# Attention products of both sequences merged and moved amid the experts in a fused two-layer tower

## The chip, the cores and the metric

The kernel runs on one core of one Trainium2 chip. The metric is the device time of one execution in microseconds, the median of several runs.

## The reference

Sixteen sequences of 128 tokens (D = 256) go through an embedding and two layers. All arithmetic is in float32.

```python
h = emb[ids] + 0.1 * sum_d mask_d * (base @ W_exp[d].T) @ W_proj[d].T     # 8 domains
n = layernorm(h)
c_kv = n @ W_dkv.T                      # latents, 128 wide
q    = n @ W_dq.T @ W_uq.T              # 16 heads of 16
h += softmax(causal(q . k_eff . c_kv / 4)) @ c_kv @ v_eff
n = layernorm(h)
h += sum_e gate_e(n) * (n @ expert_w[e]) + bias                           # 8 experts, threshold 0.1
n = layernorm(h)
u = conv4(n) @ in_w.T + in_b ; dt = tanh(n @ dt_w.T + dt_b) @ tr_w.T
s_t = silu(s_(t-1) + dt_t + ...)        # a recurrence over the 128 steps
h += out_w(s + u)
h += fp4_linear(silu(fp4_linear(layernorm(h), w_gate)) * fp4_linear(.., w_up), w_down)
```

## The kernel before, in words

**Stages.** The sequences are worked off in eight pairs (`u` = 0, 1 within a pair). A software pipeline overlaps two of them: `body(i)` runs the *back* part of pair `i` (scores, softmax, attention, gate, experts, up to the third layer norm) together with the *front* part of pair `i + 1` (embedding correction, first layer norm, latents, queries, keys, values). `body(-1)` has the front alone, `body(0)` both, `body(1)` to `body(6)` are one hardware loop and have besides the recurrence inputs of the pair before (`rec`), `body(7)` has no front; TensorE transposes feed-forward weights in its place. After the pairs come the recurrence over 128 steps and the quantized feed-forward.

**Order.** There is no planner. Each engine has its own list of calls, written out by hand, and runs its instructions in that order; semaphores order the engines among each other. An instruction that waits holds all that stand behind it on its engine.

**TensorE (L579 to L888).** In the order of a looped pair: for `u` = 0 and 1 the transposes of the next pair's raw rows `x_tok` (L575, called at L760), which wait for GpSimd's copy (`base_copied`) and for the values of the pair before; `scores(0)` for the first sequence (32 products, L597, and four causal masks, L601); `expand(0)`; `recurrence_inputs()` (L694), which waits for the convolution; half of `scores(1)`, `expand(1)`, the other half; `delta` (L711), transposes of the probabilities (L611) between those of the masked rows; `attend` (L624) with `project` between; the transposes of `n_tok`; `compress(0)` (L732: latents for queries and for keys and values of one sequence); then the gate input (L575), gate and four expert groups for each sequence (L657), each followed by the bias product (L670). Last come `compress(1)`, `heads` four times (L719: queries and keys of each sequence), `values(0)`, the transpose of the second sequence's third norm `n3_tok` and `values(1)` (L725).

**PSUM.** Four banks hold scores, probabilities and expert outputs (`pq`), two the back part (`pback`), and two the front part (`pfront[0]`, `pfront[1]`): in `before` sequence `u` uses `pfront[u]`. `scores(0)` and the expert groups wait until VectorE has read the quarter (`moe_read`).

**ScalarE (L986 to L1134)** copies from PSUM to SBUF: `xT`, `nT`, `latT`, queries, keys (two copies each, by the parity of the head), `n3T`; and it computes the 32 exps of each pair's head groups (L999) behind VectorE's maxima, and the tanh `dt_act` (L1027).

**VectorE (L1307 to L1543).** Row maxima (L1315), masking of the expanded rows (L1474), `projected` (L1400) and `deltas` (L1409, L1411) for the recurrence inputs, copies of transposed probabilities (L1321), the sum of the embedding correction (L1505), layer norm statistics (L1292, L1296) and their application (L1304), the expert mix (L1375, L1377 to L1386) and the first half of the convolution (L1421, L1424). In looped pairs it also quantizes one piece of the feed-forward weights in ten steps `weights(0)` to `weights(9)` (L1447 to L1468) that are strewn between the rest. `attend(u, 0)` on TensorE waits for `d_stored`, which `deltas` signals.

**GpSimd (L445 to L483)** has, in this order in each body: the copies of the next pair's `hidden` rows to `x_tok` (L455), the other half of the convolution (L438, L443), and for each layer norm two small steps, the sum (L425) and the power (L428) that give `rstd`. The last of them in a body is that of the third norm of the second sequence, `rstd_of(2, 1, ...)`, and the copies to `x_tok` of the next body stand behind it. In `body(0)` GpSimd also issues the gathers of the embedding rows of all later pairs between these steps.

Of the kernel before, what the change touches and what calls it, by code (L numbers as in the profile page):

```python
# [29 lines left out]
T = 128  # L30
# [44 lines left out]
def tower(nc, ids, domain_map, emb_table, w_expand, w_project, w_dq, w_uqT, w_dq_rows, w_dkv,  # L75
# [3 lines left out]
    with ctx:  # L79
# [67 lines left out]
        nT = sb("nT", [128, 2, KD, T])  # L147
        latT = sb("latT", [LATENT, 2, 2, T])
# [407 lines left out]
        def _(pe):  # L556
# [22 lines left out]
            def body(i, front, back, rec):  # L579
# [92 lines left out]
                def recurrence_transposed(u):  # L672
                    pe.wait_ge(ln_norm[2], n[u])
                    transposes(pback[u], n3_tok[:, u, :]).then_inc(xn3T_done, 1)
# [19 lines left out]
                def recurrence_inputs():  # L694
                    pe.wait_ge(n3T_ready, sequences(pe, i, 0))
                    for k in range(KD):
# [4 lines left out]
                        projected = mm(pback[0][0:STATE, 0:2 * T], inw_sb[:, k, :],  # L701
                                       mixed[:, k, :, :].rearrange("p u t -> p (u t)"),
                                       start=(k == 0), stop=(k == KD - 1), skip_group_check=True)
                        ranks = mm(pback[0][STATE:STATE + RANK, 0:2 * T], dtw_sb[:, k, :],
                                   n3T[:, :, k, TAPS - 1:], start=(k == 0), stop=(k == KD - 1), skip_group_check=True)
                    projected.then_inc(in_done, 2)
                    ranks.then_inc(rank_done, 2)
# [7 lines left out]
                def heads(u, ready, w, x, done):  # L715

                    pe.wait_ge(ready, fn[u])
                    for c in range(KD):
                        last = mm(pfront[u][:, c * T:(c + 1) * T], w[:, c * 128:(c + 1) * 128], x,  # L719
                                  start=True, stop=True)  # L720
                    last.then_inc(done, 1)

                def values(u):
                    pe.wait_ge(k_ready, fn[u])
                    mm(pfront[u][:, 0:D], latT[:, u, 1, :], veff_sb[:], start=True, stop=True).then_inc(v_done, 1)  # L725

                def compress(u):

                    pe.wait_ge(nT_ready, fn[u])
                    for c, w in enumerate((wdq_sb, wdkv_sb)):  # L730
                        for k in range(KD):
                            last = mm(pfront[u][:, c * T:(c + 1) * T], w[:, k, :], nT[:, u, k, :],  # L732
                                      start=(k == 0), stop=(k == KD - 1))
# [62 lines left out]
                if front:  # L796
                    expand(1)
                if not front:
                    weights_transposed(1)
                if back:  # L800
                    scores(1, (2, 3))
                    if rec:
                        delta(0, 2, 1, pback[1])
# [3 lines left out]
                    probs_transposed(0, 0)  # L807
                if front:
# [3 lines left out]
                if front:  # L812
                    masked_transposed(1)
                if back:
# [31 lines left out]
                if front:  # L846
                    compress(0)
# [3 lines left out]
                if back:  # L851
# [9 lines left out]
                    expert_bias(0)  # L861
                    gate(1)
                    experts(1, 0)
                    experts(1, 1)
# [20 lines left out]
                if last_pair:  # L885
# [79 lines left out]
        def _(act):  # L965
# [20 lines left out]
            def body(i, front, back, rec):  # L986
# [34 lines left out]
                def recurrence_transposed(u):  # L1021
                    act.wait_ge(xn3T_done, n[u])
# [8 lines left out]
                def queries(u):  # L1031

                    act.wait_ge(q_done, fn[u])
                    copy(qT[:, u].rearrange("p g t -> p (g t)"), pfront[u][:, 0:D], q_ready, scale=HS ** -0.5)

                def keys(u):
                    act.wait_ge(k_done, fn[u])
                    for r in (0, 1):
                        last = nc.scalar.activation(kT[:, u, r].rearrange("p g t -> p (g t)"), pfront[u][:, 0:D],
                                                    ACT.Identity, scale=of_parity[:, r:r + 1])  # L1040
                    last.then_inc(k_ready, 1)
# [16 lines left out]
                if front:  # L1058
                    for u in (0, 1):
                        act.wait_ge(baseT_done, fn[u])  # L1060
                        copy(xT[:, u].rearrange("p k t -> p (k t)"), pfront[u][:, 0:D], xT_ready)
# [20 lines left out]
                def compressed(u):  # L1082
                    act.wait_ge(lat_done, fn[u])
                    copy(latT[:, u].rearrange("p k t -> p (k t)"), pfront[u][:, 0:D], lat_ready)
# [30 lines left out]
                if back:  # L1115
                    gate_input(0)
                    gate(0)
                    gate_transposed(0)
                    gate_input(1)
                    gate(1)  # L1120
                    gate_transposed(1)
# [3 lines left out]
                if front:  # L1125
                    compressed(1)
                    queries(0)
                    queries(1)
                    keys(0)
                    keys(1)  # L1130
                if back:
                    recurrence_transposed(1)
                if last_pair:
# [87 lines left out]
        def _(dve):  # L1221
# [85 lines left out]
            def body(i, front, back, rec):  # L1307
# [119 lines left out]
                def values(u):  # L1427
                    dve.wait_ge(v_done, fn[u])
                    V.tensor_copy(v_aug[:, u, :, 0:HS],
                                  pfront[u][:, 0:D].rearrange("p (h d) -> p h d", h=HEADS)).then_inc(v_ready, 1)  # L1430
# [47 lines left out]

                if rec:
# [250 lines left out]
```

## Time and profile before

| | us |
|---|---|
| median of 3 runs | 634.71 (633.86 to 637.6) |
| profiled execution | 637.28 |
| its span, first to last instruction | 635.3 |
| TensorE matmul busy | 547.1 (86%) |
| VectorE busy | 454.4 (72%) |
| ScalarE busy | 252.2 (40%) |
| GpSimd busy | 215.3 (34%) |
| mean granted TensorE clock | 0.945 of 2.4 GHz |

The pairs take the span from about 14 to 440 us, the recurrence and the feed-forward the rest. Starts of instructions are in microseconds from the span's start. TensorE's ends are modelled, so differences of starts say more than ends. A float32 product shows as two instructions.

### The profile page before, as it was taken

To read this page: it belongs to the slowest core of one execution; us is meant where nothing else is said; L and a number is where in the kernel's file an instruction comes from. 1 tells how busy PE (TensorE), PEld (TensorE's weight loads), DVE (VectorE), ACT (ScalarE), POOL (GpSimd) and SP (SyncE) were. 2 spreads that over 40 slices of the span, in tenths; PEclk is the share of its full clock that TensorE was granted. 3 is DMA by queue.
4 is the path that set the end of the run, shared out by engine and by line. 5 is a ranking of instruction groups with operands and counts; after the bars stand their busy time and mean duration, and the time that the engine had idled before them with its cause. 6 is when DMAs were issued, how large, how long until landed. Compare 5 with 4: busy or idle time off the path is not lost.

```text
span 635.3 us, 9416 instructions
## 1 busy us (share of the span) xinstructions
PE 547.1 (86%) x3062; PEld 331.1 (52%) x3062; DVE 454.4 (72%) x1120; ACT 252.2 (40%) x781; POOL 215.3 (34%) x412
## 2 busy tenths in 40 slices
PE   2888969999998998998998998993569998989884
PEld 2665445555555555655645644741235555555553
DVE  1254757778778788788787786486678898988852
ACT  1263026326326326316416515802335444443321
POOL 6406561222213213114114113021347767664110
PEclk9879889999999999999999998996579999999997
DMA  6800100000000000000000000003300000000000
GB/s 189 248 2 27 34 25 1 2 0 0 0 0 0 0 0 0 0 0 0 0 0 0 0 0 2 1 2 68 64 1 10 17 8 18 9 18 17 9 17 17
DMA packets 13517, 12.75 MB, mean 20 GB/s; under 512 B 2795, under 2 KB 12724, under 8 KB 13492
## 3 DMA queue, kind: packets, MB, share of 16 engines
q1 hardware_dynamic: 12212, 10.34, 6.1%
q0 software_dynamic: 1280, 2.11, 1.2%
q8 instruction: 12, 0.20, 0.1%
q14 instruction: 13, 0.11, 0.1%
HBM read 8.25 MB, written 2.10 MB: 16 GB/s over the span
## 4 chain that ended last, share of the span: by engine, by line
PE 54%; DVE 12%; issue 10%; ACT 9%; POOL 8%; SPq 4%; DMA 2%; DVEq 0%; POOLq 0%; ACTq 0%
PE psum L657 13%; PE psum L919 8%; PE psum L941 5%; ACT probs L999 4%; PE psum L597 4%; SPq L383 3%; PE psum L739 3%; PE psum L575 2%; POOL rstd L428 2%; PE psum L601 2%; PE psum L750 2%; PE psum L719 2%; DVE stats L1292 2%; POOL rstd L425 2%; PE psum L732 1%
## 5 line engine op out<-in xcount | busy, mean ns | idle before, releaser
L657 PE MATMUL psum<-expw_sb,n2T 128*128 128x512 f32 x256 | 119.1, 609 | 0.0
L425 POOL TENSOR_TENSOR rstd<-meanvar,ln_eps_col 128x1 f32<-128x1 f32 x64 | 17.8, 278 | 288.2 <-DVE meanvar L1296 288.1
L919 PE MATMUL psum<-wguT,n2T 128*128 128x512 f32 (+1 forms) x192 | 82.8, 583 | 0.0
L999 ACT ACTIVATE probs<-psum,neg_max 128x128 f32<-128x128 f32 x256 | 69.1, 391 | 33.4 <-DVE neg_max L1315 33.3
L657 PEld LDWEIGHTS psum<-expw_sb,n2T 128*128 128x128 f32 x256 | 47.2, 194 | 47.6 <-issue 47.6
L941 PE MATMUL psum<-wdT,probsT 128*128 128x256 f32 x192 | 50.3, 405 | 12.7 <-ACT probsT L967 12.7
L919 PEld LDWEIGHTS psum<-wguT,n2T 128*128 128x128 f32 x192 | 38.1, 200 | 39.5 <-issue 34.4
L1315 DVE TENSOR_REDUCE neg_max<-psum 128x4 f32<-128x512 f32 x64 | 40.4, 681 | 19.7 <-PE psum L601 19.7
L967 ACT ACTIVATE probsT<-psum 128x512 f32<-128x512 f32 x72 | 37.2, 530 | 30.6 <-PE psum L611 26.0
L1143 ACT ACTIVATE probs<-u_now 64x16 f32<-64x16 f32 x128 | 27.4, 214 | 53.9 <-POOL u_now L517 37.9
L941 PEld LDWEIGHTS psum<-wdT,probsT 128*128 128x128 f32 x192 | 35.2, 196 | 25.8 <-issue 21.0
L1377 DVE SCALAR_TENSOR_TENSOR acc<-psum,g_w,acc 128x256 f32<-128x256 f32 x96 | 42.0, 479 | 7.7 <-PE psum L657 3.1
L517 POOL TENSOR_TENSOR u_now<-probs,drive 64x16 f32<-64x16 f32 x87 | 37.1, 427 | 30.0 <-ACT probs L1143 30.0
L611 PE MATMUL psum<-ident,probs 128*128 128x128 f32 x256 | 39.0, 283 | 2.6 <-ACT probs L999 2.6
L1304 DVE TENSOR_SCALAR n_tok<-hidden,meanvar,rstd 128x256 f32 (+1 forms) x48 | 20.1, 420 | 27.1 <-POOL rstd L428 27.1
L575 PE MATMUL psum<-ident,n_tok 128*128 128x128 f32 x128 | 25.2, 288 | 15.8 <-DVE n_tok L1304 11.7
L428 POOL TENSOR_TENSOR rstd<-rstd,minus_half 128x1 f32<-128x1 f32 x64 | 36.0, 562 | 5.0
L498 POOL TENSOR_TENSOR hq<-wgu_tmp,hsc 128x704 f32<-128x704 f32 x16 | 22.4, 1398 | 36.7 <-DVE wgu_tmp L1254 36.6
L597 PE MATMUL psum<-kT,qT 32*128 32x128 f32 x512 | 30.1, 298 | 4.7 <-ACT probs L999 2.4
L611 PEld LDWEIGHTS psum<-ident,probs 128*128 128x128 f32 x256 | 28.7, 143 | 10.1 <-issue 6.0
L575 PEld LDWEIGHTS psum<-ident,n_tok 128*128 128x128 f32 x128 | 15.1, 143 | 33.2 <-DVE n_tok L1304 15.5
L597 PEld LDWEIGHTS psum<-kT,qT 32*128 32x128 f32 x512 | 25.6, 200 | 12.8 <-issue 12.8
(172 smaller groups left out, 1025.7 us busy)
## 6 DMA issues: line engine op xcount, KB each, us to landing
expw_sb<-in_expert_w SPq DMA_DIRECT2D x8, 256.0 KB
expw_sb<-hidden SPq DMA_DIRECT2D x16, 128.0 KB
result<-res SPq DMA_DIRECT2D x16, 128.0 KB
w_raw<-in_w_down SPq DMA_DIRECT2D x1, 704.0 KB, 9.4
w_raw<-in_w_gate SPq DMA_DIRECT2D x1, 640.0 KB, 7.1
w_raw<-in_w_up SPq DMA_DIRECT2D x1, 640.0 KB, 8.2
wexp_sb<-in_w_expand SPq DMA_DIRECT2D x1, 256.0 KB, 3.1
wproj_sb<-in_w_project SPq DMA_DIRECT2D x1, 256.0 KB, 3.2
```

The source lines that it names most:

```text
L428: pool.tensor_tensor(rstd[:, k, u, :], rstd[:, k, u, :], minus_half[:], ALU.pow).then_inc(ln_rstd[k], 1)
L517: pool.tensor_tensor(u_now[:], gated_all[:, t, :], drive[:, t, :], ALU.add).then_inc(u_ready, 1)
L575: last = nc.tensor.transpose(bank[:, k * 128:k * 128 + rows], src[:, k * 128:(k + 1) * 128], ident[:])
L597: mm(pq[:, g, j * T:(j + 1) * T], qT[g * GROUP:(g + 1) * GROUP, u, j // 2, :], kT[g * GROUP:(g + 1) * GROUP, u, j % 2, j // 2, :], start=( ...
L611: last = nc.tensor.transpose(pq[:, g, j * T:(j + 1) * T], probs[:, u, HPQ * g + j, :], ident[:])
L657: last = mm(pq[:, g, :], n2T[:, u, k, :], expw_sb[:, k, EPQ * g:EPQ * (g + 1), :].rearrange("p e n -> p (e n)"), start=(k == 0), stop=(k = ...
L919: last = mm(pgu[u][:, c0:c1], xqT[:, u, k, :], wguT[:, k, c0:c1], start=(k == 0), stop=(k == KD - 1))
L941: last = mm(pdown, hqT[0:rows, u, k, :], wdT[0:rows, k, :], start=(k == 0), stop=(k == KI - 1))
L967: nc.scalar.activation(dst, src, ACT.Copy, **kw).then_inc(s, 1)
L999: last = nc.scalar.activation(probs[:, u, h, :], pq[:, g, j * T:(j + 1) * T], ACT.Exp, bias=neg_max[:, u, h:h + 1])
L1315: V.tensor_reduce(neg_max[:, u, HPQ * g:HPQ * (g + 1)], pq[:, g, :].rearrange("p (h k) -> p h k", h=HPQ), AX.X, ALU.max, negate=True).then ...
L1377: last = V.scalar_tensor_tensor(out=a[:, u, :], in0=p, scalar=g_w[:, u, e:e + 1], in1=a[:, u, :], op0=ALU.mult, op1=ALU.add)
```

## The change

The front part's products take both sequences at once. `compress(x, w)` makes the query latents (`x` = 0) or the key and value latents (`x` = 1) of both sequences in bank `pfront[x]`; `heads` makes queries or keys of both; `values` both sequences' values in one bank. They stand at other places of TensorE's list: the second compress behind the third expert group of the first sequence, the query heads behind its bias, the key heads behind the first expert group of the second sequence; only `values` stays at the end. ScalarE's copies (512 columns each) and VectorE's value copy follow. Both `x_tok` transposes go to `pfront[1]` and one copy takes both. The transpose of the second sequence's `n3_tok` and its copy move, in looped pairs and the last, behind `scores(0)` of the next body; the ranks' products are split from the projection's, which goes behind the first transpose of probabilities; `expand(1)` goes before `scores(1)`. On VectorE `maxima(0)` comes ahead of the convolution, `projected`, `deltas` and `weights(0)` move back, `weights(6)` ahead of the application of the first gate norm, `weights(9)` ahead of that of the second, and `values` behind `mix(1)`. GpSimd's list is as before.

```diff
@@ TensorE
-                def heads(u, ready, w, x, done):
-                    pe.wait_ge(ready, fn[u])
+                def heads(x, w, done):
+                    pe.wait_ge(lat_ready, fn[x])
                     for c in range(KD):
-                        last = mm(pfront[u][:, c * T:(c + 1) * T], w[:, c * 128:(c + 1) * 128], x, ...
+                        last = mm(pfront[x][:, 2 * c * T:2 * (c + 1) * T], w[:, c * 128:(c + 1) * 128],
+                                  latT[:, x].rearrange("p u t -> p (u t)"), start=True, stop=True)
+                def values():
+                    pe.wait_ge(lat_ready, fn[1])
+                    pe.wait_ge(q_ready, fn[1])
+                    for u in (0, 1):
+                        last = mm(pfront[0][:, u * D:(u + 1) * D], latT[:, 1, u, :], veff_sb[:], ...
+                def compress(x, w):
+                    pe.wait_ge(nT_ready, fn[1])
+                    for k in range(KD):
+                        last = mm(pfront[x][:, 0:2 * T], w[:, k, :], nT[:, :, k, :], ...
                 def expand(u):
                     pe.wait_ge(xT_ready, fn[u])
+                    if u == 0:
+                        wait(pe, v_ready, fbefore)
...
                 if front:
+                    wait(pe, k_ready, fbefore)
                     for u in (0, 1):
                         pe.wait_ge(base_copied, fn[u])
-                        wait(pe, v_ready, later(pe, fbefore, u - 1))
-                        transposes(pfront[u], x_tok[:, u, :]).then_inc(baseT_done, 1)
+                        transposes(pfront[1][:, u * D:(u + 1) * D], x_tok[:, u, :]).then_inc(baseT_done, 1)
                 if back:
                     scores(0, range(QUARTERS))
+                if rec:
+                    recurrence_transposed(1, behind=1)
                 if front:
                     expand(0)
                 if rec:
-                    recurrence_inputs()
+                    ranks_behind()
+                if front:
+                    expand(1)
                 if back:
                     scores(1, (0, 1))
-                if front:
-                    expand(1)
                     scores(1, (2, 3))
-                    if rec:
-                        delta(0, 2, 1, pback[1])
                     probs_transposed(0, 0)
+                if rec:
+                    inputs_behind()
                 if front:
                     masked_transposed(0)
                     probs_transposed(0, 1)
                     masked_transposed(1)
+                if rec:
+                    delta(0, 2, 1, pback[1])
...
-                    compress(0)
+                    compress(0, wdq_sb)
...
                     experts(0, 0)
                     experts(0, 1)
                     experts(0, 2)
+                if front:
+                    compress(1, wdkv_sb)
                     gate_transposed(0)
                     gate_input(1)
                     experts(0, 3)
                     expert_bias(0)
+                if front:
+                    heads(0, wuqT_sb, q_done)
                     gate(1)
                     experts(1, 0)
+                if front:
+                    heads(1, keff_sb, k_done)
                     experts(1, 1)
...
                 if front:
-                    compress(1)
-                    heads(0, lat_ready, wuqT_sb, latT[:, 0, 0, :], q_done)
-                    heads(1, lat_ready, wuqT_sb, latT[:, 1, 0, :], q_done)
-                    heads(0, q_ready, keff_sb, latT[:, 0, 1, :], k_done)
-                    heads(1, q_ready, keff_sb, latT[:, 1, 1, :], k_done)
-                    values(0)
-                if back:
+                    values()
+                if last_pair:
                     recurrence_transposed(1)
-                if front:
-                    values(1)
@@ ScalarE
+                    act.wait_ge(baseT_done, fn[1])
+                    nc.scalar.activation(xT[:].rearrange(...), pfront[1], ACT.Copy).then_inc(xT_ready, 2)
+                if rec:
+                    recurrence_transposed(1, behind=1)
...
                     gate(0)
+                    compressed(1)
                     gate_transposed(0)
                     gate_input(1)
+                    queries()
                     gate(1)
+                    keys()
@@ VectorE
+                if back:
+                    maxima(0, range(QUARTERS))
                 if rec:
                     convolved(0, 0, 2, 1, conv_dve, TAPS * i - TAPS)
-                if back:
-                    maxima(0, range(QUARTERS))
                 if front:
                     expanded(0)
-                if rec:
-                    projected(0, 2, 1)
-                    weights(0)
                     maxima(1, (0, 1))
                     expanded(1)
                     maxima(1, (2, 3))
+                    probs_out(0, 0)
+                    if rec:
+                        projected(0, 2, 1)
+                    probs_out(0, 1)
+                    weights(0)
                     if rec:
                         deltas(0, 2, 1, pback[1])
-                    for g in range(3):
-                        probs_out(0, g)
+                    probs_out(0, 2)
...
                     attention_out(0)
                     weights(5)
+                    weights(6)
                     ln_apply(1, 0, n[0], seq(hidden, i, 0), n2_tok[:, 0, :])
-                    weights(6)
                     weights(7)
...
                     attention_out(1)
                     weights(8)
+                    weights(9)
                     ln_apply(1, 1, n[1], seq(hidden, i, 1), n2_tok[:, 1, :])
...
                     mix(1)
+                    if front:
+                        values()
...
                     ln_apply(2, 1, n[1], seq(hidden, i, 1), n3_tok[:, 1, :])
-                if front:
-                    values(0)
-                    values(1)
-                if back:
-                    weights(9)
```

## Rows read from the trace of the kernel before

**Rows 1.** Windows, one period: us, then PE, PEld, DVE, ACT, POOL, clock, DMA

```profile
166.47:215.24 48.77, 45.58 (x308) 27.43 (x308) 38.75 (x97) 20.76 (x64) 11.60 (x21) 1.00 0.00 0
```

**Rows 2.** Timeline, TensorE: start, us, engine, line, operation, tiles, count [idle before, releaser]

```profile
174.23 0.44 PE L575 MATMUL psum<-ident,n_tok 128*128 128x128 f32 x2 [0.56 <-DVE n_tok L1304]
...
184.90 0.69 PE L670 MATMUL psum<-expb_sb,wT 8*128 8x256 f32 x2
...
186.52 1.35 PE L719 MATMUL psum<-latT,wuqT_own 128*128 128x128 f32 x8
...
190.56 0.43 PE L575 MATMUL psum<-ident,x_tok 128*128 128x128 f32 x2
...
191.87 1.17 PE L597 MATMUL psum<-kT,qT 32*128 32x128 f32 x32 [0.17 <-issue]
...
193.85 1.03 PE L739 MATMUL psum<-wexp_sb,xT 128*128 128x256 f32 x4
...
205.79 0.43 PE L624 MATMUL psum<-probsT,v_aug 128*32 128x128 f32 x8
...
215.24 0.44 PE L575 MATMUL psum<-ident,n_tok 128*128 128x128 f32 x2 [0.52 <-DVE n_tok L1304]
```

**Rows 3.** Timeline, VectorE, the same period

```profile
183.17 2.83 DVE L1377 SCALAR_TENSOR_TENSOR acc<-psum,g_w,acc 128x256 f32<-128x256 f32 x6
...
188.09 0.18 DVE L1296 BATCH_NORM_AGGREGATE meanvar<-stats 128x2 f32<-128x6 f32 x1
...
192.68 2.33 DVE L1424 SCALAR_TENSOR_TENSOR mixed<-n3T,convw_sb,mixed 128x256 f32<-128x256 f32 x3
194.94 2.47 DVE L1315 TENSOR_REDUCE neg_max<-psum 128x4 f32<-128x512 f32 x4
...
198.15 0.85 DVE L1447 TENSOR_REDUCE w_sc<-w_raw 128x44 f32 x1
...
203.96 1.87 DVE L1321 COPY probsT<-psum 128x512 f32<-128x512 f32 x3
...
207.46 0.42 DVE L1505 SCALAR_TENSOR_TENSOR hidden<-psum,hidden 128x256 f32 x1
```

**Rows 4.** Timeline, GpSimd, the seam between two pairs

```profile
188.35 0.19 POOL L425 TENSOR_TENSOR rstd<-meanvar,ln_eps_col 128x1 f32<-128x1 f32 x1 [7.29 <-DVE meanvar L1296]
188.62 0.55 POOL L428 TENSOR_TENSOR rstd<-rstd,minus_half 128x1 f32<-128x1 f32 x1
189.12 0.80 POOL L455 COPY x_tok<-hidden 128x256 f32 x2
```

**Rows 5.** Timeline, ScalarE, the exps

```profile
195.65 3.21 ACT L999 ACTIVATE probs<-psum,neg_max 128x128 f32<-128x128 f32 x12 [3.53 <-DVE neg_max L1315]
...
199.38 3.22 ACT L999 ACTIVATE probs<-psum,neg_max 128x128 f32<-128x128 f32 x12
```

**Rows 6.** Timeline, VectorE's weight steps and GpSimd's norm step beside one

```profile
166.33 0.52 DVE L1462 TENSOR_SCALAR w_mag<-w_mag 128x704 f32<-128x704 f32 x1
...
172.15 0.89 DVE L1466 TENSOR_TENSOR wgu_tmp<-wgu_tmp,w_mag 128x704 f32<-128x704 f32 x1
...
172.31 0.78 POOL L425 TENSOR_TENSOR rstd<-meanvar,ln_eps_col 128x1 f32<-128x1 f32 x1 [6.34 <-DVE meanvar L1296]
```

**Rows 7.** Timeline, TensorE's long stalls in pairs 0, 1 and 7

```profile
38.57 1.16 PE L597 MATMUL psum<-kT,qT 32*128 32x128 f32 x16 [1.60 <-issue]
...
92.00 1.11 PE L575 MATMUL psum<-ident,x_tok 128*128 128x128 f32 x4 [5.46 <-POOL x_tok L455]
93.04 2.09 PE L597 MATMUL psum<-kT,qT 32*128 32x128 f32 x32
...
390.21 0.62 PE L701 MATMUL psum<-mixed,inw_sb 128*64 128x256 f32 x2 [2.39 <-DVE mixed L1424]
```

**Rows 8.** Windows, the clock behind two of them

```profile
40.00:44.00 4.00, 4.00 (x23) 2.93 (x22) 1.71 (x3) 2.72 (x11) 0.00 (x0) 0.52 0.00 2
...
392.00:393.00 1.00, 1.00 (x4) 0.13 (x2) 0.80 (x2) 1.00 (x6) 0.00 (x0) 0.50 0.00 0
```

More of the change, by code:

```diff
@@ L670, in expert_bias, with recurrence_transposed @@
                     mm(pback[u][:, 0:D], wT[:, u, :], expb_sb[:], start=True, stop=True).then_inc(bias_done, 1)
-                def recurrence_transposed(u):
-                    pe.wait_ge(ln_norm[2], n[u])
+                def recurrence_transposed(u, behind=0):
+                    pe.wait_ge(ln_norm[2], before if behind else n[u])
                     transposes(pback[u], n3_tok[:, u, :]).then_inc(xn3T_done, 1)
@@ L692, in project_in, with ranks_behind, inputs_behind @@
                     last.then_inc(in_done, 1)
-                def recurrence_inputs():
+                def ranks_behind():
                     pe.wait_ge(n3T_ready, sequences(pe, i, 0))
+                    for k in range(KD):
+                        last = mm(pback[0][STATE:STATE + RANK, 0:2 * T], dtw_sb[:, k, :],
+                                  n3T[:, :, k, TAPS - 1:], start=(k == 0), stop=(k == KD - 1), skip_group_check=True)
+                    last.then_inc(rank_done, 2)
+                def inputs_behind():
                     for k in range(KD):
@@ L700, in recurrence_inputs @@
                             pe.wait_ge(conv_pool, conv_steps(pe, i, POOL_STEPS, 0))
[L701 to L707, printed above, removed]
+                        last = mm(pback[0][0:STATE, 0:2 * T], inw_sb[:, k, :],
+                                  mixed[:, k, :, :].rearrange("p u t -> p (u t)"),
+                                  start=(k == 0), stop=(k == KD - 1), skip_group_check=True)
+                    last.then_inc(in_done, 2)
                 def delta(u0, u1, behind, bank):
@@ L713, in delta @@
                        start=True, stop=True, skip_group_check=True).then_inc(delta_done, u1 - u0)
-                def heads(u, ready, w, x, done):
-                    pe.wait_ge(ready, fn[u])
+                def heads(x, w, done):
+                    pe.wait_ge(lat_ready, fn[x])
                     for c in range(KD):
[L719 to L733, printed above, removed]
+                        last = mm(pfront[x][:, 2 * c * T:2 * (c + 1) * T], w[:, c * 128:(c + 1) * 128],
+                                  latT[:, x].rearrange("p u t -> p (u t)"), start=True, stop=True)
+                    last.then_inc(done, 2)
+                def values():
+                    pe.wait_ge(lat_ready, fn[1])
+                    pe.wait_ge(q_ready, fn[1])
+                    for u in (0, 1):
+                        last = mm(pfront[0][:, u * D:(u + 1) * D], latT[:, 1, u, :], veff_sb[:], start=True, stop=True)
+                    last.then_inc(v_done, 2)
+                def compress(x, w):
+                    pe.wait_ge(nT_ready, fn[1])
+                    for k in range(KD):
+                        last = mm(pfront[x][:, 0:2 * T], w[:, k, :], nT[:, :, k, :],
+                                  start=(k == 0), stop=(k == KD - 1))
                     last.then_inc(lat_done, 1)
@@ L1019, in gate_transposed, with recurrence_transposed @@
                     copy(wT[:, u, :], pback[u][0:EXPERTS, 0:T], wT_ready)
-                def recurrence_transposed(u):
-                    act.wait_ge(xn3T_done, n[u])
+                def recurrence_transposed(u, behind=0):
+                    act.wait_ge(xn3T_done, before if behind else n[u])
                     copy(n3T[:, u, :, TAPS - 1:], pback[u][:, 0:D].rearrange("p (k t) -> p k t", k=KD), n3T_ready)
@@ L1058, in body @@
                 if front:
-                    for u in (0, 1):
-                        act.wait_ge(baseT_done, fn[u])
-                        copy(xT[:, u].rearrange("p k t -> p (k t)"), pfront[u][:, 0:D], xT_ready)
+                    act.wait_ge(baseT_done, fn[1])
+                    nc.scalar.activation(xT[:].rearrange("p u k t -> p (u k t)"), pfront[1], ACT.Copy).then_inc(xT_ready, 2)
+                if rec:
+                    recurrence_transposed(1, behind=1)
                 if back:
@@ L1080, in attended, with compressed @@
                     copy(yT[:, u].rearrange("p c t -> p (c t)"), pback[u][:, :], yT_ready)
-                def compressed(u):
-                    act.wait_ge(lat_done, fn[u])
-                    copy(latT[:, u].rearrange("p k t -> p (k t)"), pfront[u][:, 0:D], lat_ready)
+                def compressed(x):
+                    act.wait_ge(lat_done, fn[x])
+                    copy(latT[:, x].rearrange("p u t -> p (u t)"), pfront[x][:, 0:2 * T], lat_ready)
                 def masked_transposed(u):
@@ L1425, in convolved, with values @@
                                                    op0=ALU.mult, op1=ALU.add).then_inc(steps, 1)
[L1427 to L1430, printed above, removed]
+                def values():
+                    dve.wait_ge(v_done, fn[1])
+                    V.tensor_copy(v_aug[:, :, :, 0:HS],
+                                  pfront[0].rearrange("p (u h d) -> p u h d", u=2, h=HEADS)).then_inc(v_ready, 2)
                 def weights(k):
@@ L1535, in body @@
                         deltas(1, 2, 0, pfront[1])
[L1536 to L1540 removed]
                 if not back:
+                    values()
                     taps()
```

35 lines of the change are left out of this document (19 added, 16 removed).

## The prediction

> **What bounds the kernel now.** Read the windows of one period of the loop first: from one pair's gate input to the next is 48.77 us, and TensorE is busy for 45.58 of them at the full clock (2.4 GHz), VectorE for 38.75 [rows 1]. So TensorE is the bound, but VectorE is not far off. Then the timeline of TensorE over that period: the places where it waits are 0.56 us before the second gate input, 0.52 us before the first, and some tenths around the end of the pair [rows 2]. Then VectorE's timeline, for what its chain does when TensorE gets ahead [rows 3], and that of GpSimd, which stands between the end of one pair and the start of the next [rows 4].
>
> The seam is what the change touches. Today `mix(1)` ends on VectorE at 186.0 (183.17 + 2.83), the aggregate of its layer norm at 188.27 [rows 3], GpSimd's power at 189.17, and only then, from 189.12, does GpSimd copy the next pair's rows to `x_tok`, 0.40 us each [rows 4]. TensorE comes to the transposes of `x_tok` at 190.56, about a microsecond after the first copy, since it has 5 us of compress, heads and values to do after the last bias (184.90) [rows 2]. That work is the cover of the chain mix, norm, power, copy.
>
> **The change part by part.**
>
> 1. Merged products. 16 head products of 128 columns are two groups of 1.35 us; four of 256 columns are 1.03 us [rows 2] (each product shows as two instructions). So the heads go from 2.7 to 2.1 us, compress from as much to 2.1, values stay at about 1.05. A gain of 0.6 to 1.0 us of TensorE's time, waits for ScalarE between the heads included.
>
> 2. Moved amid the experts: one compress and two heads, 3 x 1.03 = 3.1 us. The 0.56 us wait before the second gate input hides about 0.3 of it (not all: item 5). So the last expert group of the pair ends at 184.9 + 2.8 = 187.7 instead of 184.9 [rows 2].
>
> 3. What follows on the path. `mix(1)` needs that group: two products of 0.47 us behind it [rows 3], so it ends at 188.65, not 186.0. From there to the aggregate 2.27 us as before (190.9), to the end of the power 0.90 (191.8) [rows 3, 4], and then the copies to `x_tok`, ready at 192.2 and 192.6. GpSimd's order isn't changed. TensorE has only the bias (0.6) and values (1.0) left behind its experts and stands at the `x_tok` transposes at 189.3. It waits 3.0 us, and `scores(0)` stands behind the transposes in its queue: it starts at 192.95, where it starts at 191.87 now. This is +1.1 us a pair, and the cover that hid it is the very work that moved.
>
> 4. Scores to attend. Now VectorE does the convolution (most of it in 2.33 us) before `maxima(0)` at 194.94, and exps start at 195.65 [rows 3, 5]. Afterwards the maxima come first, but the second recurrence transpose, its copy on ScalarE (0.4) and their hand-overs stand behind `scores(0)` and ahead of the exps. So: `scores(0)` ends 195.05, transpose and copy to 195.85, exps from 195.85. Twelve exps 3.2, the tanh 0.5, four exps 1.1 [rows 5]: 200.6. VectorE: maxima to 196.8, convolution 3.05 to 199.85, `expanded(0)` 0.4, so `maxima(1)` begins at 200.2 and ScalarE waits for it till 200.85; exps end at 205.2. VectorE then has maxima to 203.45 (behind `scores(1)`, which ends at 202.15), a copy (0.63), `projected` (about 0.6, taken as a copy), a copy, `weights(0)` 0.85 and `deltas` 0.7: 206.9. `attend(0,0)` waits for `deltas` and starts at 206.95 against 205.79 now [rows 2, 3]. What goes out with the old order (TensorE's short waits for the convolution, an expand between the score halves) is used up by these waits. Third copy and weights 1 to 4 (0.6 + 1.7) put VectorE at the projection's sum at 209.2, where it is at 207.46 now: +1.7 us [rows 3]. From there VectorE's chain leads: sums, norm, attention out, the norm of the gate input. 0.15 us of a wait for TensorE is saved: +1.55.
>
> 5. `weights(6)` before the first gate norm and `weights(9)` before the second. They now run while VectorE would wait for GpSimd's power. But beside `weights(8)` (0.89 us) GpSimd's first step takes 0.78 us and ends with it, where alone it takes 0.19 [rows 6, 4]. So the power can be held the same way beside `weights(6)` (0.52 [rows 6]). I bound this by 0 (it has read its input) and 0.5 us (it waits out the whole instruction) and take 0.25, the middle, on the path: +1.8 us a pair. Beside `weights(9)`, as long as `weights(8)`, it may cost 0.7, of which the inserted compress hides all but about 0.3; that is the part not gained in item 2.
> The Trainium skill, "SBUF — State Buffer", section "Who interferes with whom", says that a VectorE instruction with two SBUF inputs or in a 2-port mode and a GpSimd instruction that reads SBUF exclude each other for the whole instruction. The stretched row agrees. By that rule item 5 would cost 0.45 and the forecast would be 1 us higher.
>
> 6. The clock. A stall of 3.0 us a pair is not only its own length. From pair 0 on TensorE stalled for over 1.5 us five times in this trace; the rows show the first, the third and the fourth. Behind the 1.60 us at 38.57 the granted clock is 0.52 from 40 to 44, behind the 2.39 us at 390.21 it is 0.50 from 392 to 393, and behind the 5.46 us at 92.00 `scores(0)` takes 2.09 us for its 32 products, against 1.17 [rows 7, 8, 2]. That is the lower of its two levels, 1.2 GHz. The short waits of the period don't do this: its clock is 1.00 [rows 1]. So I expect the half clock behind the new stall, where `scores(0)` (0.92 more for the products, about 0.8 for the masks, the same ratio) and the transpose stand on the path. Bounds: 0, if it falls elsewhere or doesn't come, and 3.4, if the expands and the second scores are slowed too (a stretch at 1.2 GHz covers 7 us from 40 on). I take 1.6, nearest to `scores(0)` alone.
> The Trainium skill, "TensorE: Matmul & The Clock Gate", section "HAM oscillation — how this bites in real kernels", names only longer gaps than this as what lets the clock fall. The row of 2.39 us speaks against that; by the rule the forecast would be the second case below.
>
> **Sum.** Per period 1.8 + 1.6 = +3.4 us; five periods lie between pair 1's gate input and pair 6's: +17.0. Before them: in pair 0, `expand(1)` fills the 1.60 us wait and the half clock behind it goes (40 to 44 and on), -2.5; the inserted 3.1 us delay the last power of pair 0, behind which GpSimd issues its last gathers, and TensorE already waits 5.46 us for the copy behind those, +3.1 in full; and pair 1's steps of items 4 and 5 (which has the half clock already) +1.3. That is +1.9. In the last pair there are no `x_tok` transposes: `scores(0)` starts 1.3 us sooner, and exps no longer wait for the convolution (TensorE's 2.39 us there [rows 7]). `weights(0)` is absent too. I work out `attend(0,0)` 1.6 us sooner; bounds 0 and 3: -1.6. Together +17.3 us. The profiled execution took 637.28 (span 635.3), the median of the runs is 634.71; the same difference on the median gives 652.0.
>
> **The rivals.**
> - Stall without the half clock: 5 x 1.8 + 1.9 - 1.6 = +9.3, 644.0. For it: that how the stall falls counts (0.3 to 0.6 us waits do nothing). Against it: even 1.60 us did. Chance 0.17.
> - The clock falls and also slows the experts, since TensorE waits again, 1.2 us, at the first gate input. Experts are wholly TensorE's: up to 5.2 a period in all, +26, 661 and above. Chance 0.10, at the upper edge.
> - The seam's loss is made good: with maxima first, exps start 1 us sooner after `scores(0)`, and if `maxima(1)` isn't held by the convolution (were VectorE's 3.05 us near 1.9, as four steps of the 0.47 us in `mix` [rows 3] would be), +1.1 is met by -1.1: 636, within 1%. Against: GpSimd's own convolution runs at the same time, as now. Chance 0.12.
> - Faster: `scores(0)` isn't held by the copies. Then it starts at 189.85, 2.0 us sooner; half of it is lost to VectorE's order, 1.0 a period stays: -5 -1.6 -1 = -7.6, 627. It decides at one point: `x_tok` has to be copied by 189.3, 3 us before mix, norm and power allow. Against it is the order of GpSimd's queue, for it that the merged products could be much shorter than 1.03 us (they'd have to be nearly nothing). That the change doesn't act as it says is a part of this. Chance 0.08.
>
> **How the numbers follow.** The forecast, stall with half clock, has 0.53: 645 to 661. With 0.17, 0.10, 0.12 and 0.08 for the rivals: faster by over 1% 0.08, within 1% 0.12, slower 0.80 (1% is about what a measurement tells from no change). Range 638 to 662: it leaves out the faster case and most of the clock in the experts.
>
> **What would show it.** In the profile after: a wait of TensorE's transposes of `x_tok` (L575) for GpSimd's copy (L455) of about 3 us in each of the looped pairs; no such wait before the last pair. Granted clock 0.5 for some microseconds behind it. ScalarE idle about 0.3 us ahead of the fifth quarter's exps; attend waiting for `drive`. Period 52.2 us (50.6 without the clock). It is wrong if the transposes wait for under 1 us, if the period is below 49.5, or if the experts' stretch is not 2.8 us longer.

## Result and profile after

The changed kernel takes 655.56 us (median, 653.02 to 656.88), the one before 634.29 in the same series: ratio 1.034 (1.029 to 1.039), slower, as forecast (652.0, 638 to 662). Profiled executions: 656.56 against 637.28 us, +19.3; medians: +21.3. Over all series the kernel before ran in 628.6 to 640.9 us, and the ratios leave out runs of more than 1.5% above the fastest of their kernel.

TensorE over one looped pair, the timeline (start, duration, line, tiles, count, idle before and releaser), to be held against [rows 2]:

```profile
171.15 0.44 PE L576 MATMUL psum<-ident,n_tok 128*128 128x128 f32 x2 [0.92 <-DVE n_tok L1325]
...
178.08 1.03 PE L740 MATMUL psum<-nT,wdkv_sb 128*128 128x256 f32 x4
...
179.58 0.44 PE L576 MATMUL psum<-ident,n_tok 128*128 128x128 f32 x2 [0.36 <-DVE n_tok L1325]
...
192.37 0.69 PE L671 MATMUL psum<-expb_sb,wT 8*128 8x256 f32 x2
192.99 1.13 PE L733 MATMUL psum<-veff_sb,latT 128*128 128x256 f32 x4
196.92 1.12 PE L576 MATMUL psum<-ident,x_tok 128*128 128x128 f32 x4 [2.80 <-POOL x_tok L456]
197.96 2.09 PE L598 MATMUL psum<-kT,qT 32*128 32x128 f32 x32
...
207.63 1.16 PE L598 MATMUL psum<-kT,qT 32*128 32x128 f32 x16 [0.66 <-ACT probs L1015]
...
213.82 0.43 PE L625 MATMUL psum<-probsT,v_aug 128*32 128x128 f32 x8 [0.43 <-DVE drive L1432]
...
223.69 0.44 PE L576 MATMUL psum<-ident,n_tok 128*128 128x128 f32 x2 [0.93 <-DVE n_tok L1325]
```

Behind the bias and `values` TensorE is done at 194.1 and stands before the `x_tok` transposes until 196.92. `scores(0)` behind them takes 2.09 us for its 32 products. What it waited for is in VectorE's and GpSimd's timelines [rows 3, 4]:

```profile
192.48 0.88 DVE L1398 SCALAR_TENSOR_TENSOR acc<-psum,g_w,acc 128x256 f32<-128x256 f32 x2 [1.17 <-PE psum L658]
...
195.43 0.18 DVE L1317 BATCH_NORM_AGGREGATE meanvar<-stats 128x2 f32<-128x6 f32 x1
```

```profile
195.69 0.19 POOL L426 TENSOR_TENSOR rstd<-meanvar,ln_eps_col 128x1 f32<-128x1 f32 x1 [9.28 <-DVE meanvar L1317]
195.96 0.55 POOL L429 TENSOR_TENSOR rstd<-rstd,minus_half 128x1 f32<-128x1 f32 x1
196.47 0.80 POOL L456 COPY x_tok<-hidden 128x256 f32 x2
```

VectorE waited 1.17 us for the last expert group (before it was behind, not waiting), then came mix, norm, power and copy. The waits of TensorE, summed (us, times, longest), say that one place grew:

```profile
PE psum L576 <- POOL x_tok L456: 23.3, 6, 9.3
PE psum L957 <- ACT probsT L983: 12.4, 16, 0.8
PE psum L576 <- DVE n_tok L1325: 11.9, 15, 1.7
```

Before, the first of these was 5.5 us, once. Now it is 9.3 us in that same place, in the body of pair 1, where the copy waits for the last gathers, and 2.8 us in each of the five looped pairs behind it. Last the windows, one for each of the five periods (TensorE, its weights, VectorE, ScalarE, GpSimd busy, then the granted clock), and of three stretches in them, to be held against [rows 1]:

```profile
117.48:171.15 53.67, 48.27 (x292) 28.19 (x292) 38.55 (x96) 20.10 (x60) 12.03 (x21) 0.94 0.00 0
171.15:223.69 52.54, 47.31 (x292) 28.12 (x293) 38.43 (x96) 19.98 (x60) 12.03 (x21) 0.94 0.00 0
223.69:277.23 53.54, 48.12 (x293) 28.27 (x293) 38.74 (x96) 20.19 (x60) 11.91 (x21) 0.94 0.00 0
277.23:329.76 52.53, 47.18 (x292) 28.04 (x293) 38.41 (x96) 19.88 (x60) 12.04 (x21) 0.94 0.00 0
329.76:383.39 53.63, 49.16 (x292) 28.96 (x293) 38.38 (x96) 19.75 (x60) 12.03 (x21) 0.90 0.00 0
...
154.00:157.00 3.00, 3.00 (x20) 1.93 (x17) 1.98 (x4) 2.54 (x11) 0.00 (x0) 0.61 0.00 0
196.00:202.00 6.00, 5.08 (x42) 3.38 (x43) 2.05 (x5) 0.60 (x1) 1.27 (x3) 0.50 0.00 0
...
329.76:335.00 5.24, 5.20 (x17) 2.88 (x18) 3.23 (x13) 0.74 (x3) 0.00 (x0) 0.73 0.00 0
```

The period is 53.18 us in the mean against 48.77, and the clock 0.94 and less in every period, where it was 1.00. From 196 to 202, around the end of the stall, it is at the lower level (1.2 GHz) throughout. In the last period the start of the experts is slowed too (0.73 from 329.76 to 335.00), although TensorE works nearly without a gap there. TensorE's busy time rises by 1.6 to 3.6 us a period (45.58 to between 47.18 and 49.16) though there are fewer instructions: a part of the work runs at half the clock.

### The profile page after: what moved, and what is told of

The parts are those of the page before. It is cut to its first block, busy times and chain, and to the rows that moved or that the text cites. A ratio compares the mean times of both kernels' runs of the same rounds, so it can differ in the third digit from the quotient of the medians.

```text
span 654.6 us, 9150 instructions
## 1 busy us (share of the span) xinstructions
PE 551.4 (84%) x2934; PEld 329.7 (50%) x2934; DVE 452.4 (69%) x1112; ACT 245.9 (38%) x749; POOL 217.2 (33%) x412
## 4 chain that ended last, share of the span: by engine, by line
PE 48%; DVE 15%; issue 12%; ACT 10%; POOL 8%; SPq 4%; DMA 2%; POOLq 0%; DVEq 0%; ACTq 0%
PE psum L658 14%; PE psum L935 7%; ACT probs L1015 5%; PE psum L957 5%; PE psum L598 3%; SPq L384 3%; PE psum L576 3%; POOL rstd L429 3%; PE psum L724 2%; PE psum L602 2%; DVE stats L1313 2%; PE psum L612 2%; POOL rstd L426 2%; DVE n_tok L1325 1%; PE psum L646 1%
## 5 line engine op out<-in xcount | busy, mean ns | idle before, releaser
L658 PE MATMUL psum<-expw_sb,n2T 128*128 128x512 f32 x256 | 121.0, 612 | 0.0
L429 POOL TENSOR_TENSOR rstd<-rstd,minus_half 128x1 f32<-128x1 f32 x64 | 41.8, 653 | 5.0
L598 PE MATMUL psum<-kT,qT 32*128 32x128 f32 x512 | 34.3, 343 | 6.2 <-ACT probs L1015 4.9
L598 PEld LDWEIGHTS psum<-kT,qT 32*128 32x128 f32 x512 | 29.2, 239 | 14.5 <-issue 14.5
L612 PEld LDWEIGHTS psum<-ident,probs 128*128 128x128 f32 x256 | 30.8, 149 | 8.5 <-issue 7.6
```

Source lines behind the costliest of these rows:

```text
L429: pool.tensor_tensor(rstd[:, k, u, :], rstd[:, k, u, :], minus_half[:], ALU.pow).then_inc(ln_rstd[k], 1)
L598: mm(pq[:, g, j * T:(j + 1) * T], qT[g * GROUP:(g + 1) * GROUP, u, j // 2, :], kT[g * GROUP:(g + 1) * GROUP, u, j % 2, j // 2, :], start=( ...
L612: last = nc.tensor.transpose(pq[:, g, j * T:(j + 1) * T], probs[:, u, HPQ * g + j, :], ident[:])
L658: last = mm(pq[:, g, :], n2T[:, u, k, :], expw_sb[:, k, EPQ * g:EPQ * (g + 1), :].rearrange("p e n -> p (e n)"), start=(k == 0), stop=(k = ...
```

## Experiments

Each kernel is the changed one with the edit shown, if not said otherwise. Results are medians and ratios to the kernel before in the same series.

**Copies first.** GpSimd's last norm step of a looped pair goes behind the next pair's copies (in pair 7's body its own stays where it was):

```diff
                 if rec:
+                    rstd_of(2, 1, before)
                     convolved(i, 1, 0, 2)
...
-                    rstd_of(2, 1, n[1])
+                    if not front:
+                        rstd_of(2, 1, n[1])
```

> The changed kernel with one edit on GpSimd: in looped pairs the last norm step of the pair before is issued behind the copies to x_tok instead of ahead of them. Theory (the seam: TensorE waits 2.8 us for the copies, and the half clock follows from that wait): the wait goes, scores(0) starts 3 us sooner in the period at the full clock, VectorE's order then gives a part of it back; period 48 to 49 us instead of 53.2, time 628 to 636. Rival (the loss lies in VectorE's new order and in the convolution and the copy behind scores(0)): TensorE then waits at the third norm's transpose instead, about as long, and the time stays above 648.

Measured: 627.49 us, 0.989 (0.985 to 0.993). TensorE's timeline at the seam, and the windows of a period:

```profile
185.69 0.60 PE L578 MATMUL psum<-ident,x_tok 128*128 128x128 f32 x4
186.22 1.17 PE L600 MATMUL psum<-kT,qT 32*128 32x128 f32 x32
187.33 1.04 PE L604 MATMUL psum<-causal_bf,ident_bf 128*128 128x512 bf16 x4
188.75 0.44 PE L578 MATMUL psum<-ident,n_tok 128*128 128x128 f32 x2 [0.39 <-DVE n_tok L1327]
```

```profile
162.88:210.87 47.99, 44.96 (x293) 26.53 (x293) 38.75 (x96) 19.89 (x60) 11.71 (x21) 1.00 0.00 0
```

The wait is gone, `scores(0)` covers the norm all but 0.39 us, and the clock stays full. The order of the norm step and the copies in GpSimd's queue was 28 us, 26 of them in the five periods (53.18 against 47.97 in the mean). Without it the rest of the change gains 1.1% on the median, a little more than expected. The kernel before ran in 629.1 to 640.9 us in this series, so against its fastest run the gain is only 1.6 us. The rival, that VectorE's order is the loss, falls.

**Products in the stall.** The wait stays, but TensorE works in it:

```diff
                     wait(pe, k_ready, fbefore)
+                    if rec:
+                        for _ in range(10):
+                            mm(pfront[1], ident_bf[:], causal_bf[:].rearrange("p h q -> p (h q)"),
+                               start=True, stop=True)
```

> The changed kernel with ten bf16 products of 512 columns (masks into a free bank, results unused, about 2.4 us) in the place of TensorE's wait for x_tok, in the looped pairs. The wait for the copy stays as long in sum (2.8 us), only TensorE isn't idle in it. Theory (half of the loss is the clock that falls behind the stall): no stretch at half clock behind the seam, period 53.2 down to 50.8, time 655.6 down by 11 to 14, 642 to 645. Rival (the clock falls only behind longer gaps, or for other reasons): no gain, 654 to 658.

Measured: 646.0 us, 1.021 (1.015 to 1.028), 9.6 us less than the changed kernel for 60 products more. `x_tok` comes as late as ever; TensorE still idles 0.64 us. The windows of two periods:

```profile
167.55:217.93 50.38, 47.15 (x302) 27.59 (x302) 38.21 (x96) 19.95 (x60) 11.98 (x21) 1.00 0.00 0
217.93:269.98 52.05, 48.79 (x303) 28.28 (x303) 38.44 (x96) 20.16 (x60) 11.97 (x21) 0.97 0.00 0
```

Four of the five periods are 50.4 us at the full clock, one fell to half for a while: 50.73 in the mean, and 646.0 is 1 us above what was expected. So of the 4.41 us by which a period of the changed kernel is longer than before, 1.6 (50.4 against 48.77) are waiting and order and 2.8 (53.18 against 50.4) are the clock. What pulled the clock down was TensorE's idleness in the stall, not the change's instructions; that it also falls without such a stall, the second window shows.

**Weights back.** `weights(6)` and `weights(9)` at their old places:

```diff
                     weights(5)
-                    weights(6)
                     ln_apply(1, 0, n[0], seq(hidden, i, 0), n2_tok[:, 0, :])
+                    weights(6)
...
                     weights(8)
-                    weights(9)
                     ln_apply(1, 1, n[1], seq(hidden, i, 1), n2_tok[:, 1, :])
...
+                if back:
+                    weights(9)
```

> The changed kernel with weights(6) and weights(9) at their old places. Theory (a VectorE instruction on SBUF holds up GpSimd's power beside it: 0.84 and 1.21 us instead of 0.55): both powers take 0.55 again, the first gate input comes 0.3 us sooner and TensorE's 0.36 us wait before the second goes: 0.65 us a period in six periods, -4 us, 651.5. If only the start matters (the instruction waits for its turn anyway): under 1 us. Both weight steps then run in VectorE's other gaps and cost nothing.

Measured: 645.52 us, 1.020 (1.013 to 1.027): -10, not -4. GpSimd's powers and the weight steps beside them in the changed kernel, then the powers with the weights back:

```profile
169.72 0.53 DVE L1483 TENSOR_SCALAR w_mag<-w_mag 128x704 f32<-128x704 f32 x1
169.81 0.84 POOL L429 TENSOR_TENSOR rstd<-rstd,minus_half 128x1 f32<-128x1 f32 x1
...
177.77 0.89 DVE L1489 TENSOR_TENSOR w_raw<-wgu_tmp,w_sc 128x704 f32 x1
177.87 1.21 POOL L429 TENSOR_TENSOR rstd<-rstd,minus_half 128x1 f32<-128x1 f32 x1
```

```profile
168.15 0.55 POOL L429 TENSOR_TENSOR rstd<-rstd,minus_half 128x1 f32<-128x1 f32 x1
...
175.90 0.55 POOL L429 TENSOR_TENSOR rstd<-rstd,minus_half 128x1 f32<-128x1 f32 x1
```

The mechanism holds: both powers were held up, by 0.29 and 0.66 us. The Trainium skill, "SBUF — State Buffer", section "Who interferes with whom", has this rule (the two exclude each other for the whole instruction). The rows agree in that both powers end only behind the weight step beside them; by the rule I had reckoned 0.45 for the first, and the row says 0.29. But the time fell by more than twice the forecast. Periods are 51.64 and 50.81 us in turn, each with one stretch at half clock, a long and a short one. The changed kernel has periods of 52.54 with one long stretch and of 53.6 with two short ones (the second is the 0.61 from 154 to 157 above). Like against like, the long stretch costs 0.9 us less than 52.54, near the 0.65 expected; the rest is that no period has a second stretch. Why it is gone was not tried by itself.

**Merged in place.** `compress(1)`, `heads` and their copies back at the end of the pair, merged:

```diff
                     experts(0, 2)
-                if front:
-                    compress(1, wdkv_sb)
...
                     expert_bias(0)
-                if front:
-                    heads(0, wuqT_sb, q_done)
...
                     experts(1, 0)
-                if front:
-                    heads(1, keff_sb, k_done)
...
                 if front:
+                    compress(1, wdkv_sb)
+                    heads(0, wuqT_sb, q_done)
+                    heads(1, keff_sb, k_done)
                     values()
```

> The changed kernel with compress(1), both heads and their copies back at the end of the pair: merged for both sequences, but not amid the experts. Theory (the place costs, not the merge): the last expert group ends 2.8 us sooner in the period, so mix, norm and copies do too, and TensorE arrives at x_tok with the copies ready or within 0.5 us of it; no half clock; period 48.0 to 48.8, time 626 to 634. Rival (the merged products or VectorE's order cost): above 645.

Measured: 631.55 us, 0.998 (0.995 to 1.001). The windows:

```profile
162.33:210.70 48.37, 44.66 (x292) 26.73 (x292) 38.19 (x96) 20.06 (x60) 11.92 (x21) 1.00 0.00 0
```

The period is 48.5 in the mean, the clock full. Merging takes 0.9 us off TensorE's busy time (45.58 before [rows 1]), of which the period keeps 0.25 (48.77 before), and costs nothing; the place amid the experts, with the order of GpSimd's queue, is the loss.

**Third norm in its pair.** The second recurrence transpose and its copy on ScalarE are turned back, ahead of the `x_tok` transposes (TensorE's list is shown):

```diff
-                if rec:
-                    recurrence_transposed(1, behind=1)
...
                 if front:
                     values()
+                if back:
+                    recurrence_transposed(1)
```

> The changed kernel with the second recurrence transpose and its copy back at the end of their own pair, between values and the transposes of x_tok; all else as changed. Theory: it waits for the norm that is ready just before the copies are, so the stall is as long (2.6 to 3.0 us, now ahead of this transpose), scores(0) starts 0.2 to 0.4 us later, and exps no longer stand behind the copy: 651 to 657. Rival (turning it behind the scores is what costs): below 645.

Measured: 657.05 us, 1.039 (1.031 to 1.048), at the upper end of what was expected. Then the same together with the copies first:

> Both edits at once: GpSimd's copies ahead of the last norm step, and the second recurrence transpose at the end of its own pair. Theory (turning the transpose behind the scores is needed just as the order of the copies is, since both stand behind the same norm and either holds TensorE's queue): the stall of 2.9 us is back, now for the norm, with the half clock behind it: 650 to 657. Rival (the copies alone were the price, the turned transpose is worth nothing): within 3 us of the copies-first run's 627.5.

Measured: 650.34 us, 1.029 (1.022 to 1.035). Its seam:

```profile
189.65 0.44 PE L578 MATMUL psum<-ident,n_tok 128*128 128x128 f32 x2 [2.89 <-DVE n_tok L1326]
```

GpSimd's copies are done at 179.7 here, ten microseconds early, and TensorE waits as long, now for the norm. Both edits are needed: the transpose behind the scores *and* the copies ahead of the norm. The change made the first of them; alone it is worth next to nothing (657.05 against 655.56), since the copy stands behind the same norm. The copies alone are worth nothing in the looped pairs either: the five periods are 52.18 us in the mean without them and 52.32 with them. The 6.7 us between 657.05 and 650.34 lie elsewhere, 5.1 of them (61.27 against 56.13 in the profiles) between the gate inputs of pairs 0 and 1, where the last gathers, and the copy behind them, no longer wait for that norm.

**The kernel before, copies first.** The same edit on GpSimd:

> The kernel before with GpSimd's copies to x_tok ahead of the last norm step, the edit that mends the changed kernel. Theory: before, TensorE arrives about a microsecond behind the first copy, so there is nothing to gain: within 0.5% of 634.3. Rival (the order of GpSimd's queue costs in both): 628 or less. In pair 1 the copies stand before a norm step and wait for the gathers, which may shift some tenths.

Measured: 637.2 us, 1.007 (1.002 to 1.012); its profiled period is 48.97 against 48.77. There was nothing to gain, and 0.2 us a pair are lost. 637.2 is within 0.5% of the 634.3 named, but the ratio in the same series, 1.007, is a little outside; its runs lie from 629.3 to 640.5 and those of before from 628.6 to 640.7, so I make nothing of it. The rival (628 or less) falls. TensorE's list here is that of the kernel before, so its profile also shows what differs from run to run (below).

**Rearranged.** Copies first, and VectorE's weight steps where it waits:

```diff
+                    if rec:
+                        deltas(0, 2, 1, pback[1])
                     weights(0)
-                    if rec:
-                        deltas(0, 2, 1, pback[1])
...
                     weights(3)
-                    weights(4)
...
-                    weights(5)
-                    weights(6)
                     ln_apply(1, 0, n[0], seq(hidden, i, 0), n2_tok[:, 0, :])
-                    weights(7)
+                    weights(4)
+                    weights(5)
+                    weights(6)
...
-                    weights(8)
-                    weights(9)
+                    weights(7)
                     ln_apply(1, 1, n[1], seq(hidden, i, 1), n2_tok[:, 1, :])
...
                     for g in range(QUARTERS):
+                        if u == 1 and g > 1:
+                            weights(6 + g)
                         dve.wait_ge(moe_done[g], n[u])
```

> The kernel of the copies-first run with VectorE's weight steps put where it waits: weights(4) to (6) behind the first gate norm, (7) before the second, (8) and (9) between the last groups of mix(1), where VectorE waits 0.76 and 1.17 us for the experts; deltas ahead of weights(0). Theory: the gate inputs lose 0.29 and 0.36 us of waiting, attend its 0.43; period 48.0 down to 46.9 to 47.3, time 627.5 down to 620 to 624. Rival (TensorE is full and what is saved turns up as another wait): 626 to 628. A step too long for its gap would make the seam later: 629 and above.

Measured: 618.98 us, 0.980 (0.972 to 0.987), a little less than expected and better than either kernel. The windows of two periods, and the first gate input:

```profile
112.14:158.42 46.28, 44.73 (x293) 26.58 (x293) 38.73 (x96) 19.76 (x61) 10.52 (x21) 1.00 0.00 1
158.42:205.99 47.57, 46.08 (x293) 27.31 (x293) 38.87 (x96) 19.94 (x61) 10.52 (x21) 0.96 0.00 0
```

```profile
158.42 0.44 PE L578 MATMUL psum<-ident,n_tok 128*128 128x128 f32 x2 [0.28 <-DVE n_tok L1327]
```

Three of five periods are 46.3 us; two, at 47.6, have a half-clock stretch (0.96) though no wait of theirs is over a microsecond. The moved steps were not tried one by one, so what each is worth is open.

## Why the prediction was right, and where its sizes were off

The mechanism came as forecast: the copy behind mix, norm and power, the stall, the half clock behind it, in every looped pair; the experiments show that each link is needed. The sizes did less well, and the total is partly luck.

- Item 1, merging: 45.58 to 44.66 us of TensorE busy in place, within the 0.6 to 1.0 reckoned. The working was less good: what it calls 16 head products and four are instructions (eight products and two), and it puts the compress products before at 2.7 us like the heads, where the rows of one sequence take 0.99 us from their start to that of the heads (186.52 [rows 2]), so about 2.0 for both:

```profile
185.53 0.71 PE L732 MATMUL psum<-nT,wdq_sb 128*128 128x128 f32 x4
186.08 0.61 PE L732 MATMUL psum<-nT,wdkv_sb 128*128 128x128 f32 x4
```

- Items 2 and 3, the seam: from the first gate input to the last bias 21.22 us against 18.43, +2.8 as forecast; forecast a stall of 3.0 us, measured 2.80 in each of five looped pairs. `scores(0)` starts 26.81 us after the gate input against 25.40: +1.4, forecast +1.1; the rest is the transposes at half clock.
- Item 4: `attend` waits 0.43 us for `deltas`, as forecast. Of the 0.3 us that ScalarE was to idle ahead of the fifth quarter's exps, about 0.1 is there. At the full clock, by the products-in-stall run, items 3 to 5 make 1.6 us a period, forecast 1.8.
- Item 5: held up 0.29 us on the path, taken as 0.25; beside `weights(9)` 0.66 (0.7), which leaves TensorE a wait of 0.36 us (0.3).
- Item 6, the clock, was mis-sized: I took 1.6 us, nearest to `scores(0)` alone, and it is 2.8. From `scores(0)` to `attend` the shown period takes 15.86 us against 13.92; the period before it, with the second stretch, 17.13. The upper bound of 3.4 was the nearer one. The rival that the clock stays full (644) fell.
- The evidence of item 6 was weaker than it looked. In the profile of before with the copies first, the same waits stand at the same places of TensorE's list, 1.59 us in pair 0 and 2.40 us in pair 7, and the clock behind both is 1.00, where it was 0.52 and 0.50 [rows 8]. Pair 0 there:

```profile
37.17 1.16 PE L599 MATMUL psum<-kT,qT 32*128 32x128 f32 x16 [1.59 <-issue]
```

```profile
38.00:46.00 8.00, 7.08 (x62) 5.14 (x59) 4.79 (x8) 6.62 (x24) 0.00 (x0) 1.00 0.00 1
```

- "Before them", +1.9, was -0.2, and its first term was hit by luck. Pair 0's first gate input is at 57.40 against 59.88, the -2.5 forecast, and `expand(1)` did shorten the wait (0.74 and 0.42 us instead of 1.60). But the half clock that was to go with it stayed (the window below), and 2.1 of the 2.5 us were there before the wait, at the start of pair 0's `scores(0)`. First the kernel before, then the changed one and its window:

```profile
33.97 1.17 PE L597 MATMUL psum<-kT,qT 32*128 32x128 f32 x32
```

```profile
31.84 1.17 PE L598 MATMUL psum<-kT,qT 32*128 32x128 f32 x32
...
40.00:44.00 4.00, 4.00 (x21) 3.30 (x20) 2.22 (x4) 2.95 (x13) 0.00 (x0) 0.50 0.01 2
```

With TensorE's old order, in the profile of before with the copies first, that gate input is at 56.53, earlier than in the changed kernel. So the start differs by 2 to 3 us from run to run: the profile of before has stretches at half clock from 26 to 30 and from 40 to 47 us, and the one with the copies first has none from 14 to 56. The 3.1 us inserted delay pair 0's last norm step by only 1.4 us, counted from the gate input (25.49 against 24.06): the first twelve expert instructions take 7.09 us against 8.03, since less of the half clock falls on them.
- Behind pair 6's gate input the changed kernel gave back 2.5 us, forecast 1.6. It is what is left (19.3 - 21.8, the shift at that gate input, 383.39 against 361.54). 2.1 of it lie between the gate inputs of pairs 6 and 7 (46.11 against 48.23 us). The kernel before with the copies first takes 47.12 us there, with no half clock behind its wait, so about 1 us of the 2.1 may be the run and not the change.

The sum by measured terms is -0.2 + 5 x 1.6 + 5 x 2.8 - 2.5 = +19.3; it closes because the last term is the remainder. Against my 17.3 the clock makes +6, items 3 to 5 make -1, the start -2 and the end -0.9. That the errors partly cancel is luck.

## What to carry to other kernels

Work between the end of a chain and the next consumer is cover; before moving it forward, follow the chain through *every* engine's queue and look for an instruction of the next stage that stands behind it for no reason of data. Two consumers behind one norm have to be freed together, or nothing is gained: here either alone left the periods at 52 to 53 us, and both gave 48. A stall on TensorE can cost more than its length shows: here 2.80 us of it came with 2.8 us for the clock. When a profile is compared with another, look first whether a kernel repeats the stretch in question from run to run; pair 0 did not.

## What the runs showed of the hardware

- The clock's share of a 2.8 us stall is 2.8 us a period, as long as the stall and longer than what the stall itself puts on the path (1.6 with all else). Behind or in each of the 20 stalls of 2.8 to 2.9 us of the looped pairs (five each in the changed kernel and in the runs weights back, third norm in its pair, and both edits at once) the granted clock falls to 0.50.
- With shorter waits it is not settled. Behind 1.60 us it was 0.52 in one profile and behind 1.59 us at the same place 1.00 in another; behind 2.39 us 0.50 and behind 2.40 us 1.00. In three of five periods of the changed kernel there are two stretches below the full clock, and in the rearranged kernel it fell twice where no wait was over a microsecond. What decides was not found here.
- TensorE's idle time can be filled with products whose results nobody reads: 60 of them gained 9.6 us.
- GpSimd's power takes 0.55 us by itself. Beside a VectorE instruction on SBUF it took 0.84 us and ended 0.40 us behind that instruction (170.25 and 170.65), though it started 0.44 us before its end; beside the longer one it took 1.21 us and ended 0.42 us behind (178.66 and 179.08).
